# Second product of a mixture-of-experts layer: w2's high and low parts side by side in one 512-column matmul, each sum in a bank of its own

## What is computed

```python
xg = x_pad[dispatch]                                            # rows of each expert, 256 wide
h = _gelu(jnp.einsum('ecd,edf->ecf', xg, w1) + b1[:, None, :])  # 256 -> 1024
y = jnp.einsum('ecf,efd->ecd', h, w2) + b2[:, None, :]          # 1024 -> 256
wy = y * g[..., None]
out = segment_sum(wy, dispatch)
```

## Time and profile before

| | us |
|---|---|
| runs of the kernel before: median (lowest to highest) | 962.76 (962.26 to 964.36) |
| the profiled execution's own time | 961.9 |
| its span in the profile | 959.7 |
| TensorE busy in the span | 930.3 |
| ScalarE busy | 538.0 |
| VectorE busy | 469.6 |
| GpSimd busy | 394.0 |

### The profile page before, as it was taken

One profiled execution on the slowest core, in us unless ns is written; L12 is line 12 of the kernel. 1 busy time (PEld: TensorE's weight loads), 2 busy tenths in 40 slices (PEclk: granted clock), 3 DMA queues, 4 the chain that ended last, 5 costly groups with the idle time before them and its releaser, 6 DMA issues.

```text
span 959.7 us, 19188 instructions
## 1 busy us (share of the span) xinstructions
PE 930.3 (97%) x6403; PEld 889.7 (93%) x6404; DVE 469.6 (49%) x1083; ACT 538.0 (56%) x1231; POOL 394.0 (41%) x419
## 2 busy tenths in 40 slices
PE   6999799999999999999999999999999999999994
PEld 3566599999999999999999999999999999999993
DVE  4488676645534554435444454355344543343341
ACT  5977554656645564556555555466546555555551
POOL 0000113554544545534535545445445445355433
PEclk9999999999999999999999999999999999999997
DMA  9576553252532243322522342325323223223222
GB/s 329 181 226 218 196 192 81 52 133 45 135 48 43 48 84 96 46 40 51 134 37 50 50 120 52 48 41 136 44 45 45 43 51 45 38 51 50 33 35 32
DMA packets 53559, 82.18 MB, mean 86 GB/s; under 512 B 6736, under 2 KB 42576, under 8 KB 53136
## 3 DMA queue, kind: packets, MB, share of 16 engines
q0 software_dynamic: 26496, 36.76, 23.9%
q1 hardware_dynamic: 25472, 44.44, 13.7%
q10 hardware_dynamic: 1552, 0.53, 0.2%
HBM read 54.17 MB, written 35.93 MB: 94 GB/s over the span
## 4 chain that ended last, share of the span: by engine, by line
PE 86%; issue 12%; DMA 1%; POOL 1%; ACT 0%; DVE 0%; POOLq 0%; DVEq 0%
PE bank L555 14%; PE bank L556 14%; PE bank L557 14%; PE bank L542 13%; PE bank L543 13%; PE bank L544 13%; PE bank L532 3%; DMA sb_xg<-hidden,sb_gather_ids 1%; PE bank L499 1%; POOL out_rows L383 0%; POOL sb_xg L370 0%; PE bank L466 0%; PE bank L464 0%; ACT sb_h_raw L726 0%; ACT sb_h_hi L726 0%
## 5 line engine op out<-in xcount | busy, mean ns | idle before, releaser
L726 ACT ACTIVATE sb_h_raw<-bank,sb_b_now 128x384 f32<-128x384 f32 x368 | 214.8, 584 | 285.2 <-PE bank L544 267.5
L1073 DVE TENSOR_TENSOR sb_h_lo<-sb_h_raw,sb_h_hi 128x384 fp32r<-128x384 f32 x368 | 204.9, 557 | 297.0 <-ACT sb_h_hi L726 286.2
L555 PE MATMUL bank<-sb_w_hi,sb_h_hi 128*128 128x256 f32 x1104 | 315.1, 285 | 0.0
L556 PE MATMUL bank<-sb_w_lo,sb_h_hi 128*128 128x256 f32 x1104 | 310.8, 282 | 0.0
L557 PE MATMUL bank<-sb_w_hi,sb_h_lo 128*128 128x256 f32 x1104 | 310.2, 281 | 0.0
L383 POOL DMA_INDIRECT out_rows<-sb_y,sb_add_ids x138 | 224.9, 1630 | 67.8 <-POOL sb_add_ids L380 36.2
L542 PE MATMUL bank<-sb_xt_hi,sb_w_hi 128*128 128x384 f32 x736 | 249.6, 339 | 0.5 <-ACT sb_h_hi L726 0.5
L544 PE MATMUL bank<-sb_xt_hi,sb_w_lo 128*128 128x384 f32 x736 | 248.8, 338 | 0.0
L543 PE MATMUL bank<-sb_xt_lo,sb_w_hi 128*128 128x384 f32 x736 | 248.8, 338 | 0.0
L726 ACT ACTIVATE sb_h_hi<-bank,sb_b_now 128x384 fp32r<-128x384 f32 x368 | 212.4, 577 | 0.0
L556 PEld LDWEIGHTS bank<-sb_w_lo,sb_h_hi 128*128 128x128 f32 x1104 | 208.2, 189 | 0.0
(11 more groups left out here) (133 smaller groups left out, 585.9 us busy)
## 6 DMA issues: line engine op xcount, KB each, us to landing
sb_w_raw<-in_w SPq DMA_DIRECT2D x16, 1024.0 KB
hidden<-sb_rows SPq DMA_DIRECT2D x4, 2112.0 KB, 9.4
sb_x<-in_x_t SPq DMA_DIRECT2D x16, 512.0 KB, 4.4
out_rows<-in_x SPq DMA_DIRECT2D x16, 512.0 KB, 5.6
sb_xg<-hidden,sb_gather_ids POOLq DMA_INDIRECT x138
out_rows<-sb_y,sb_add_ids POOLq DMA_INDIRECT x138
sb_b<-in_b SPq DMA_DIRECT2D x1, 1024.0 KB, 5.3
hidden<-sb_empty SPq DMA_DIRECT2D x3, 132.0 KB, 8.2
```

What stands on the lines that cost most here:

```text
L555: pe.matmul(y, hi, w_hi[u][:, cols], start=(f == 0 and s != 1), stop=False, skip_group_check=True)
L556: pe.matmul(y, hi, w_lo[u][:, cols], start=False, stop=False, skip_group_check=True)
L726: ins = act.activation(h, h_bank[f % H_BANKS][:, 0:SLOTS], ACT.Gelu_apprx_tanh, bias=b1_now[u][:, f:f + 1])
L1073: dve.tensor_tensor(h_lo[f % RING][:, :], h_raw[f % RING], h_hi[f % RING][:, :].bitcast(F32), ALU.subtract).then_inc(h_ready, 1)
```

## The change

w1 and w2 are kept in separate buffers; w2's high and low part of a chunk lie side by side (`w2_both[u][:, f, 0, :]` and `[:, f, 1, :]`), 512 columns in a row. `second_product` issues two matmuls for a tile in place of three: `h_hi` by both parts, 512 columns, into a whole bank; and `h_lo` by the high part, 256 columns, into the bank's upper half. The sum of a tile is then in two halves of a bank. VectorE adds the lower half to the bias (three instructions), then the upper half to that (three more), which now carries `y_read`. The three sums need three whole banks: 2, 6 and 7. Bank 7 held the positions and counts, so VectorE copies the 24 counts to SBUF in `find_slots(3)` (`counts_e`, semaphore `pos_read`), later readers take them from there, and TensorE waits for `pos_read` once, in block 0.

```diff
-        w_hi = [sb(f"w_hi{u}", [P, 2 * WCOLS], F32R) for u in range(2)]
-        w_lo = [sb(f"w_lo{u}", [P, 2 * WCOLS], F32R) for u in range(2)]
+        w1_hi = [sb(f"w1_hi{u}", [P, WCOLS], F32R) for u in range(2)]
+        w1_lo = [sb(f"w1_lo{u}", [P, WCOLS], F32R) for u in range(2)]
+        w2_both = [sb(f"w2_both{u}", [P, FC, 2, D], F32R) for u in range(2)]
+        counts_e = sb("counts_e", [P, 3 * E])
+        def w_raw_piece(i):
+            cols = w_raw[:, i * PIECE:(i + 1) * PIECE]
+            return cols if i < PIECES // 2 else cols.rearrange("p (c d) -> p c d", d=D)
+        def w_part(u, i, part):
+            if i < PIECES // 2:
+                return (w1_hi, w1_lo)[part][u][:, i * PIECE:(i + 1) * PIECE]
+            c = (i - PIECES // 2) * (PIECE // D)
+            return w2_both[u][:, c:c + PIECE // D, part, :]
...
-        y_bank = [bank[2][:, 0:D], bank[2][:, 256:256 + D], bank[6][:, 0:D]]
+        y_bank = [bank[2], bank[6], bank[7]]
...
             def second_product(u, f):
-                cols = slice(WCOLS + f * D, WCOLS + (f + 1) * D)
+                both = w2_both[u][:, f, :, :].rearrange("p v d -> p (v d)")
                 for s in range(SUBS):
                     hi = h_hi[f % RING][:, s * P:(s + 1) * P]
                     lo = h_lo[f % RING][:, s * P:(s + 1) * P]
-                    y = y_bank[s]
-                    pe.matmul(y, hi, w_hi[u][:, cols], start=(f == 0 and s != 1), stop=False, skip_group_check=True)
-                    pe.matmul(y, hi, w_lo[u][:, cols], start=False, stop=False, skip_group_check=True)
-                    mm = pe.matmul(y, lo, w_hi[u][:, cols], start=False, stop=(f == FC - 1), skip_group_check=True)
+                    pe.matmul(y_bank[s][:, :], hi, both, start=(f == 0), stop=False)
+                    mm = pe.matmul(y_bank[s][:, D:2 * D], lo, w2_both[u][:, f, 0, :], start=False, stop=(f == FC - 1))
...
                     if f == 3:
                         pe.wait_ge(y_read, b * SUBS + SUBS)
+                        if isinstance(b, int) and b == 0:
+                            pe.wait_ge(pos_read, 1)
...
-                act.copy(w_hi[u][:, cols], w_raw[:, cols]).then_inc(w_hi_done, 1)
+                act.copy(w_part(u, i, 0), w_raw_piece(i)).then_inc(w_hi_done, 1)
...
-                dve.tensor_tensor(w_lo[u][:, cols], w_raw[:, cols], w_hi[u][:, cols].bitcast(F32),
+                dve.tensor_tensor(w_part(u, i, 1), w_raw_piece(i), w_part(u, i, 0).bitcast(F32),
                                   ALU.subtract).then_inc(w_lo_done, 1)
...
                 n = mark(dve.tensor_tensor(slot_e[:, :, :], pos, base3, ALU.add))
+                if s == SETS - 1:
+                    dve.tensor_copy(counts_e[:, :], pos_bank[:, COUNT_AT:COUNT_AT + 3 * E]).then_inc(pos_read, 1)
...
                 for s in range(SUBS):
                     dve.wait_ge(y_free, b * SUBS + 1)
-                    dve.wait_ge(y_done, b * SUBS + max(s + 1, 2))
-                    dve.tensor_tensor(y[s][:, :], y_bank[s], b2_sb[:, bass.ds(e * D, D)],
-                                      ALU.add).then_inc(y_read, 1)
+                    dve.wait_ge(y_done, b * SUBS + (s + 1))
+                    dve.tensor_tensor(y[s][:, :], y_bank[s][:, 0:D], b2_sb[:, bass.ds(e * D, D)], ALU.add).then_inc(y_summed, 1)
+                for s in range(SUBS):
+                    dve.wait_ge(y_summed, b * SUBS + (s + 1))
+                    dve.tensor_tensor(y[s][:, :], y[s][:, :], y_bank[s][:, D:2 * D], ALU.add).then_inc(y_read, 1)
```

More of the change, by code:

```diff
@@ L235, in build @@
         third_saved = sem("third_saved")
+        y_summed = sem("y_summed")
+        pos_read = sem("pos_read")
         early_step = sem("early_step")
@@ L541, in first_product @@
                     rows = slice(k * SLOTS, (k + 1) * SLOTS)
-                    pe.matmul(h, w_hi[u][:, cols], xt_hi[:, rows], start=(k == 0), stop=False)
-                    pe.matmul(h, w_hi[u][:, cols], xt_lo[:, rows], start=False, stop=False)
-                    mm = pe.matmul(h, w_lo[u][:, cols], xt_hi[:, rows], start=False, stop=(k == KC - 1))
+                    pe.matmul(h, w1_hi[u][:, cols], xt_hi[:, rows], start=(k == 0), stop=False)
+                    pe.matmul(h, w1_hi[u][:, cols], xt_lo[:, rows], start=False, stop=False)
+                    mm = pe.matmul(h, w1_lo[u][:, cols], xt_hi[:, rows], start=False, stop=(k == KC - 1))
                 mm.then_inc(h_open, 1)
             def second_product(u, f):
-                cols = slice(WCOLS + f * D, WCOLS + (f + 1) * D)
+                both = w2_both[u][:, f, :, :].rearrange("p v d -> p (v d)")
                 for s in range(SUBS):
@@ L947, in known @@
             def known(at, n):
-                return pos_bank[:, at:at + 1].to_broadcast([P, n])
+                return at.to_broadcast([P, n])
             FEW = 2 * SUBS
@@ L962, in list_two_blocks @@
                 dve.tensor_tensor(early_ids[:, few], lower_list[:, few], slot_sb[:, 2, few], ALU.add)
-                early_mark(dve.tensor_tensor(short[:, few], early_sb[:, few], known(HALF_AT, FEW), ALU.is_gt), 1)
+                early_mark(dve.tensor_tensor(short[:, few], early_sb[:, few], known(pos_bank[:, HALF_AT:HALF_AT + 1], FEW), ALU.is_gt), 1)
                 early_mark(dve.scalar_tensor_tensor(spare[:, few], short[:, few], -NO_SLOT,
@@ L970, in list_third_block @@
                 dve.wait_ge(listed, LAST_SET)
-                dve.tensor_tensor(short[:, more], early_sb[:, more], known(THIRD_AT, SUBS), ALU.is_gt)
-                early_mark(dve.tensor_tensor(early_ids[:, more], known(HALF_AT, SUBS), slot_sb[:, 0, more], ALU.is_le), 3)
+                dve.wait_ge(pos_read, 1)
+                dve.tensor_tensor(short[:, more], early_sb[:, more], known(counts_e[:, 2 * E:2 * E + 1], SUBS), ALU.is_gt)
+                early_mark(dve.tensor_tensor(early_ids[:, more], known(counts_e[:, E:E + 1], SUBS), slot_sb[:, 0, more], ALU.is_le), 3)
                 dve.tensor_tensor(short[:, more], short[:, more], short[:, SUBS:FEW], ALU.max)
```

6 lines of the change are left out of this document (2 added, 4 removed).

## The result

| | us |
|---|---|
| changed kernel: median of 18 runs (lowest to highest) | 965.91 (964.39 to 969.37) |
| kernel before on the same chip: median of 18 runs | 962.49 (961.05 to 964.36) |
| ratio (95% interval) | 1.0037 (1.0028 to 1.0047) |
| the profiled execution after, and its span | 966.5 and 964.8 |

The change made the kernel slower, by 3.4 us. The forecast was 952.7 us, faster; both its sign and its range were wrong.

A forecast was written before the change was run, and what follows sets the result against it. TensorE was taken to bound the kernel, with no wait left in the 46 blocks. Matmuls -10.8 us and the end +0.7 gave -10.1 us, so 952.7 us; forecast range 947 to 958, eight in ten 947 to 960.

The forecast's parts named there:

- I take 15.7 ns: TensorE's second product: a 512-column matmul costs 15.7 ns beyond its columns, 229.0 ns; 9.8 ns saved a tile, 10.8 us in all.
- the bound of 18.7: 512-column matmul: its time beyond its columns grows as from 256 to 384 columns, giving 232.0 ns and 7.5 us saved.
- The rival of the surplus that goes with the columns: A 512-column matmul costs as much as two of 256: 963.5 us, or 960.7 with a small fixed part; chance 0.10.
- 17.46 was forecast: Sign in the profile after: a block's period falls from 17.693 to 17.46 us.
- The far bound's surplus: 512-column matmul: 1.3 ns beyond its columns, from float32 records of that width; 214.6 ns each, 26.7 us saved.
- I cost the wait at nothing: Block's end: the next second product's wait for VectorE's y adds costs nothing, with 0.49 us left to TensorE.
- The rival of the new wait: Slower side: second adds over 0.50 us apart stall TensorE at each block's first second product; 980 us at 0.70; chance 0.08.
- The split moves: VectorE's split of chunk 1 ends 3.15 us after the last chunk's second product starts; TensorE wants it at about 5.2.
- The multiplies, and with them `y_ready`, come some 0.6 us later: Block's end: gate multiplies come some 0.6 us later; GpSimd has most of a 17.7 us block for the scatter.
- Block 0, bank 7 and the splitting of the weights at nothing: Copying the counts, TensorE's new wait in block 0 and w2's outputs in two runs of 256 cost nothing.
- The end, 0.7 us: Behind the last matmul: the first multiply comes 2.6 us after the last second product's start, 0.7 us more than before.
- VectorE's busy time: Sign in the profile after: VectorE's busy time near 527 us, with 138 more adds of 0.418 us, 58 us.

The follow-up runs named there:

- experiment 1: Changed kernel with the wide matmul split again into 256-column ones (three a tile), keeping its three banks and six adds: 967.97 us, ratio 1.006.
- experiment 7: Changed kernel with banks 2 and 7 exchanged between the first and third tile: 965.36 us in a single run.
- experiment 8: Changed kernel with a chunk's three tiles taken in the order 2, 1, 0 in all chunks but the last: 965.5 us in a single run.
- experiment 9: Changed kernel with a one-column ScalarE copy ahead of each pair of GELUs: 965.71 us, ratio 1.0035; put on top of the repaired kernel: 961.69 us.
- experiment 10: The repaired kernel with the 256-column matmul ahead of the 512-column one in every tile: 952.0 us, ratio 0.9898.
- Experiment 2: Changed kernel without the three upper-half adds, so low-part products don't reach the output: 959.68 us, ratio 0.997.
- experiment 3: Changed kernel with VectorE's loop over pairs of experts written out: 963.61 us, ratio 1.0004 against the kernel before.
- experiment 4: Changed kernel with VectorE's pair loop written out and GpSimd's scatter-id copy moved ahead of its wait for y: 960.56 us, ratio 0.9983.
- experiment 11: The repaired kernel with a chunk's three wide matmuls first, then the three narrow ones, in all chunks but the last: 956.31 us, ratio 0.9933.
- the repaired kernel: Changed kernel with VectorE's pair loop written out and GpSimd's scatter-id copy ahead of its wait: 960.56 us; with the narrow matmul first as well, 952.0 us.
- experiment 6: Changed kernel with only GpSimd's scatter-id copy moved ahead of its wait, VectorE's loop kept: 969.28 us, ratio 1.0072.

## Why the prediction was wrong, point by point

Two steps failed: the price of the wide matmul, which was mis-sized, and the waits for VectorE and GpSimd, which were put at nothing. The bound engine and the sum at the end of the kernel held.

**"I take 15.7 ns, that of the nearest float32r width, 384: 229.0 ns. A tile saves ... 9.8 ns, in all 10.8 us."** This term was mis-sized. In an ordinary pair the wide matmul takes about 233 ns, a surplus of some 20 ns, just beyond the bound of 18.7 that came from letting the surplus grow. A pair of 0.351 us saves 7 ns against three matmuls, 7.7 us in all. I had treated the value nearest in width as the likely one, although the two widths of the trace already showed the surplus rising with the columns; continuing that rise would have been the nearer guess. The rival of the surplus that goes with the columns had the right direction and was given 0.10.

**The same step, its second fault.** It gave every pair one price. The third pair of chunks 0 to 2 costs 0.035 us more, 4.8 us in all, and the 48 matmuls of 384 columns in a block take 0.016 us more together, 0.7 us in all. With that 7.7 becomes 2.2, which is what the periods say. This was in none of the bounds. Experiments 1, 7, 8, 9 and 10 show what it hangs on: it needs the wide matmul (1), it belongs to the place in time and not to bank or tile (7, 8), it doesn't follow a small shift of ScalarE (9), and it goes if the narrow matmul comes first (10). Why that order removes it stays open, as does why only three of eight chunks show it. One difference that no run isolates: with the wide matmul first, the narrow one adds to the bank's upper half, which the wide one has written last. With that order the period is 17.45 us, where 17.46 was forecast, but not by the forecast's working: the pair is still 0.352 us, and the rest comes from matmuls of 384 columns, which are 173.9 ns apart in the mean in place of 175.8. Two errors cancel there, and the match is no support for 229 ns. (The far bound's surplus was written as 1.3 ns where its row gives 1.6; nothing hangs on it.)

**"I cost the wait at nothing" (for `y_read`).** Right in the ordinary block. The second adds are 0.33 us apart, as forecast, and only one block of 46 waits for them, by 0.24 us; there the adds were late because GpSimd was. The rival of the new wait named this place and this pace, and neither was the loss.

**"The split moves ... to about T + 2.6 and ends 3.15, while TensorE wants it ... at about T + 5.2."** The sum was right for an ordinary block and missed the two blocks in which VectorE pauses behind the gate multiplies. What stands behind the pause is the split of the chunk after that one, and its cover had been nearly spent: the pause of 3.25 us was in the trace of before, marked "issue", and left 0.37 us. I had not looked for it, because the busy share and the waits of TensorE showed nothing. The multiplies came 0.59 us later, as forecast, and the pause grew by 1.53 us, which no row of before could tell and no run explains. This cost 5.1 of the 6.5 us, some 1.5 of them by a clock that fell after the idle time. Experiment 2 shows that the second adds are needed for this loss, and experiment 3 that the pause is.

**"The multiplies, and with them `y_ready`, come some 0.6 us later; GpSimd has most of a 17.7 us block."** Argued from a mean again. The copy that opens the scatter slid into a run of VectorE's without gaps and took up to 2.42 us for 0.28. The two late blocks that I put down to GpSimd made 1.4 of the 6.5 us. Experiments 3 and 4 differ only in this copy's place: 963.61 and 960.56 us, ratios 1.0004 and 0.9983. For the block at 582 us (0.5 us) the trace shows the chain from the copy to TensorE; for the one at 214 us (0.9 us) the cause stays open, since experiments 9 and 11 have it without the long copy.

**Block 0, bank 7 and the splitting of the weights at nothing.** The first blocks' distances are 20.92, 20.11 and 18.96 us against 21.04, 20.12 and 18.92 before. Right.

**The end, 0.7 us.** Right, with 0.6 measured. VectorE and GpSimd at the end, beside the earlier trace rows:

```profile
949.27 1.08 DVE L1124 TENSOR_TENSOR sb_y<-bank,sb_b 128x256 f32<-128x256 f32 x3 [1.97 <-PE bank L569]
950.27 1.07 DVE L1127 TENSOR_TENSOR sb_y<-sb_y,bank 128x256 f32<-128x256 f32 x3
951.26 0.87 DVE L1132 TENSOR_SCALAR sb_y<-sb_y,sb_gates 128x256 f32<-128x256 f32 x3
```

The last second product starts at 948.65, and the first multiply 2.61 us behind it, where 2.6 was forecast.

**VectorE's busy time**, 510.1 us where 527 were forecast: I summed single durations (418 ns), while queued adds overlap in the records (three in 1.07 us). It changed nothing else.

**The chances.** All terms costed at nothing were taken as certain, and the 0.08 for the slower side was tied to one mechanism. The single rival on that side had the wrong place, and the sum had no term for blocks unlike the one of the earlier trace rows.

## What to carry to other kernels

Slack is not the mean of a stage: before work is added to an engine that is covered, look along its whole timeline for its rare pauses (here two of 3.3 us, marked "issue", at the turn of a loop) and ask whether the cover holds there too. A wider matmul saves less than the count of instructions suggests, and the order of a wide and a narrow one can be worth more than the merge: 17.693 us a block before, 17.645 with the merge and 17.45 with the merge and the other order. When a change that shortens the bound engine brings nothing, take away one new stall at a time: the merge with its order is worth 1.0% in the repaired kernel (952.0 us), and nothing in the kernel that still has its small delays on half-idle engines (961.82 us).

## What the runs showed of the hardware that was not expected

- A float32r matmul occupies 119.4, 175.7 and about 233 ns at 256, 384 and 512 columns; over its columns at 2.4 GHz that is 12.7, 15.7 and some 20 ns.
- The order of a 256- and a 512-column matmul on the same tile moved a block by 0.2 us, and moved the 384-column matmuls around it as well (176.5 to 177.0 ns in the mean behind the slow pairs, and 173.3 to 173.9 there with the narrow one first).
- VectorE's turn of a loop showed pauses from 3.17 to 5.17 us in otherwise nearly equal programs, and none with the loop written out.
- A GpSimd copy of 128x3 numbers took 0.18 to 2.42 us; the longest were all beside runs of VectorE subtractions without gaps, and ended within 0.05 us of the end of one of them.
- After an idle stretch of 1.72 us TensorE's granted clock fell to its lower level until 447.2 us, some 3 us; after 1.40 us in another block it stayed at the higher one. In experiment 6 it stayed there after 2.09 us and fell after 2.11 us, in the same execution. There the fall cost 1.6 us.
